# One turn of a software pipeline reordered: top-8 searches at its end, decoding at the start of the next, one-hot rows made a turn ahead

## The chip, the cores and the metric

The kernel runs on one core of one Trainium2 chip. Its time is the device time of one execution in microseconds (us). Each execution covers the whole layer, for 4096 tokens, from the inputs in HBM to the output in HBM.

## The reference

The layer has two parts, each added to its input with a gate (tanh of a scalar):

```python
x = x + tanh(g_xattn) * xattn(layernorm(x), ctx)      # 16 heads of 16, 64 keys, causal, softmax
h = silu(layernorm(x) @ W_up.T + b_up) @ W_down.T + b_down        # 256 -> 1024 -> 128
q = h @ W_q.T                                                     # 2 x 8 heads x 64
sim = einsum('pbthn,hkpn->pbthk', q, keys)                        # 16 rows of 45 per token
scores, idx = top_k(sim, 8)
all_scores = sx[..., :, None] + sy[..., None, :]                  # 8 x 8 sums per head
sc, pk = top_k(all_scores, 8); indices = ix * 45 + iy at pk       # 64 experts per token, of 2048
z = silu(einsum('btd,bthkd->bthk', h, down_embed[indices]) * softmax(sc))
x = x + tanh(g_ffn) * einsum('bthk,bthkd->btd', z, up_embed[indices])
```

The kernel never fetches a chosen expert's row. It computes h against all 2048 experts (a table of 128 rows r by 16 columns c), picks 64 values for each token with one-hot matrices, and spreads the 64 coefficients back into the same table before one dense product with `up_embed`.

## The kernel before

The 4096 tokens are 32 tiles of 128. The work on a tile is cut in five stages, and a turn i of the pipeline works on five tiles at once: L (tile i: load, first layernorm), A (i-1: attention), Fw (i-2: up and down projections, dense product z, similarities), B (i-3: router) and Ct (i-4: gather, coefficients, output). 36 turns are written out; 28 in the middle have all five stages. `turn(L, A, Fw, B, Ct, side)` exists once for each engine and is the order in which that engine takes its work. Engines meet through one semaphore for each step (`S["name"]`); a step waits with `wait(name)` for its own tile's count, with `free(name)` for the previous tile's. Nothing reorders the queues: a waiting instruction holds all that stands behind it on its engine.

What the texts below name:

- TensorE (PE): `up` L858, values L941, `gather(k)` L827 for k = 0 to 3 (16 pairs of tokens each: 48 matmuls of 32 columns, z in three bf16 parts against the one-hot rows `hot_rT`, into two PSUM banks in turn, so `gather(2)` waits for VectorE to have copied bank 0, `gather(3)` for bank 1), `scores` L868 between `gather(0)` and `gather(1)`, `probs_T` L901, down projection L960, `dense` L883, `scatter(k)` L845, output projection of the attention L997 (`wo_pe`), the product with `up_embed` L1004, the transposes L1010 of the second layernorm's result (`xn2_ok`) and L1018 of the router's columns and weights (`sm_pe`), and, opening the next turn, the transposes L919 of the first layernorm's result (`xn_ok`).
- VectorE (DVE): one-hot columns `hot_c` L630; `hot_T(part)` L602, which turns broadcast expert rows into the one-hot `hot_rT`; `gathered(k)` L589; `scores_max` L617; `up_silu` L623; coefficients `uc` L610; searches: `top` L798 (16 maxima over 45), `sums` L669, `best` L682, `besti` L691 and `topi` L702 (the indices); decoding: `ab_i` L731 to `r_h` L773 and `dif` L762, which turn found positions into expert numbers; `sm_in` L776 to L787 (softmax and what is transposed in L1018); `x1` L718 and the second layernorm's statistics to L728; `xn` L752 (second layernorm), `xn` L793 (first one); `x1k` L803, the turn's last.
- ScalarE (ACT): copies out of PSUM, tanh and exp; `top_rep` L541 and `ex` L544 serve the decoding, `sm_ok` L553 to L558 copies the result of L1018.
- GpSimd (POOL): `zl` L362 and `zll` L365 (the low bf16 parts of z), and two small powers, `rstdb` L368 and `rstd` L371, for the two layernorms.
- SyncE (SP) issues all DMAs on one queue: `xt`, `ct` in; the router's rows `r_h` out to HBM (L313); their broadcast to 128 partitions (L321, two of 1024 KB); the transposes of `hot_rT` to `hot_r` for the scatter (L309); the output (L326).

Before the change a turn ends on VectorE with decoding, `top` and `x1k`; `r_h` goes to HBM and comes back broadcast at the start of the next turn, where `hot_T(0)` and `hot_T(1)` wait for it, ahead of `gathered(0)`.

Of the kernel before, what the change touches and what calls it, by code (L numbers as in the profile page):

```python
# [27 lines left out]
SLOTS = RH * K8  # L28
# [9 lines left out]
def flamingo_layer(nc, x, ctx_512, g_xattn, g_ffn, Wq, Wkv, Wout, W_up, b_up, W_down, b_down, W_r,  # L38
# [10 lines left out]
    with es:  # L49
# [3 lines left out]
        def sem(name):  # L53
# [129 lines left out]
            "uc0 uc1 uc2 w_pe0 w_pe1 w_pe2 w_pe3 w_sb0 w_sb1 w_sb2 w_sb3 out_pe y_ok y_out0 y_out1 settled"  # L183
        ).split()}

        class Tile:

            def __init__(self, eng, t, count, pair):  # L190
                self.eng, self.t, self.pair, self.count = eng, t, pair, count
                self.later = not isinstance(t, int)

            def wait(self, name):
                self.eng.wait_ge(S[name], self.count(1))

            def wait_apart(self, name):

                self.wait(name)
                self.eng.sem_inc(S["settled"], 1)  # L200

            def wait_dma(self, name, n=1):

                self.eng.wait_ge(S[name], 16 * n * self.count(1))
# [4 lines left out]
            def free(self, name, n=1):  # L209
                if self.later or self.t > 0:  # L210
                    self.eng.wait_ge(S[name], n * self.count(0))

            def free_apart(self, name, n=1):
                if self.later or self.t > 0:
                    self.eng.wait_ge(S[name], n * self.count(0))
                    self.eng.sem_inc(S["settled"], 1)

            def free2(self, name, apart=False):
                if self.later or self.t > 1:
                    self.eng.wait_ge(S[name], self.count(-1))  # L220
                    if apart:
                        self.eng.sem_inc(S["settled"], 1)

            def free_dma_side(self, name):
                if self.later or self.pair > 0:
                    self.eng.wait_ge(S[name], 16 * self.pair)
# [3 lines left out]
        def one_turn(eng, turn, i):  # L230

            tiles = [Tile(eng, i - d, lambda k, t=i - d: t + k, (i - d) // 2) if 0 <= i - d < TILES else None
                     for d in range(DEPTH)]
            turn(*tiles, (i - 1) % 2)
# [61 lines left out]
        def _(sp):  # L296
            def turn(L, A, Fw, B, Ct, side):
                if L:
                    ls = 1 - side
                    L.free2("x1_ok", apart=True)  # L300
                    sp.dma_start(xt[:, ls, :], x_d[bass.ds(L.t, 1), :, :].rearrange("a p d -> p (a d)")).then_inc(S[f"x_in{ls}"], 16)
                    L.free2("xT_pe", apart=True)
                    sp.dma_start(ct[:, ls, :], ctx_d[bass.ds(L.t, 1), :, :].rearrange("a p d -> p (a d)")).then_inc(S[f"ctx_in{ls}"], 16)
                if Ct:
                    Ct.free_apart("w_pe3")
                    for part in range(2):
                        qs = slice(part * Q // 2, (part + 1) * Q // 2)
                        Ct.wait_apart(f"hotrT{part}")
                        sp.dma_start_transpose(hot_r[:, qs, :], hot_rT[:, qs, :].rearrange("r q s -> r (q s)")).then_inc(S[f"hotr_in{part}"], 16)  # L309
                if B:  # L310
                    B.wait_apart("rh_ok")
# [3 lines left out]
                    sp.sem_inc(S["settled"], 1)  # L315
                    B.free_apart("g_pe3")
                    for part in range(2):
                        B.free_apart(f"hotr_in{part}", 16)
                    for part in range(2):
# [3 lines left out]
                                     ).then_inc(S[f"rows_in{part}"], 16)  # L323
                if Ct:
                    Ct.wait_apart("y_ok")
                    sp.dma_start(out_d[bass.ds(Ct.t, 1), :, :].rearrange("a p d -> p (a d)"), x1k[:, 1 - side, :])\  # L326
                        .then_inc(S[f"y_out{1 - side}"], 16)
# [26 lines left out]
        def _(pool):  # L354
            def turn(L, A, Fw, B, Ct, side):
                if B:

                    B.wait("z_sb3")
                    B.free2("g_pe3")
                    if Ct:  # L360
                        Ct.wait("uc2")
                    nc.gpsimd.tensor_tensor(zl[:, side, :, :], z[:, side, :, :], top_half(z[:, side, :, :]), ALU.subtract).then_inc(S["zl_ok"], 1)  # L362
                if B:
                    B.wait("zl_ok")
                    nc.gpsimd.tensor_tensor(zll[:, side, :, :], zl[:, side, :, :], top_half(zl[:, side, :, :]), ALU.subtract).then_inc(S["zll_ok"], 1)  # L365
# [3 lines left out]
                if L:  # L369
                    L.wait("eps_ok")  # L370
                    nc.gpsimd.tensor_tensor(rstd[:, :], veps[:, :], minus_half[:, :], ALU.pow).then_inc(S["rstd_ok"], 1)  # L371
# [43 lines left out]
        def _(act):  # L415
            def turn(L, A, Fw, B, Ct, side):
# [57 lines left out]
                if A:  # L474
# [62 lines left out]
                if B:  # L537

                    B.wait("top_i")
                    B.free("pick_ok")  # L540
                    copy(top_rep[:, :, :, :], topi[:, :, :].rearrange("p l a -> p a l").unsqueeze(3).to_broadcast([128, K8, 2 * RH, K8]), "rep_ok")  # L541
                    B.wait("dif_ok")
                    B.free("p_ok")
                    nc.scalar.activation(ex[:, :, :], dif[:, :, :], ACT.Exp).then_inc(S["ex_ok"], 1)  # L544
# [4 lines left out]
                if B:  # L549

                    B.wait("sm_pe")
                    B.free2("hotc")
                    for half in range(2):  # L553
                        rows, cols = slice(half * 64, half * 64 + 64), slice(half * Q, half * Q + Q)
                        src = bG1[rows, 0:256].rearrange("p (n t) -> p n t", n=2)
                        nc.scalar.activation(c_sm[rows, side, :, :], src[:, 0, cols].unsqueeze(2).to_broadcast([64, Q, 2]), ACT.Copy)
                        last = nc.scalar.activation(p_sm[rows, side, :], src[:, 1, cols], ACT.Copy)
                    last.then_inc(S["sm_ok"], 1)  # L558
# [17 lines left out]
        def _(dve):  # L576
            def turn(L, A, Fw, B, Ct, side):
# [20 lines left out]
                def hot_T(part):  # L598

                    qs = slice(part * Q // 2, (part + 1) * Q // 2)  # L600
                    Ct.wait_dma(f"rows_in{part}")
# [26 lines left out]
                if Ct:  # L628
# [37 lines left out]
                if B:  # L666

                    B.wait("top_v")
                    nc.vector.tensor_tensor(sums[:, :, :, :],  # L669
                                            top[:, 0:RH, :].unsqueeze(3).to_broadcast([128, RH, K8, K8]),  # L670
                                            top[:, RH:2 * RH, :].unsqueeze(2).to_broadcast([128, RH, K8, K8]), ALU.add).then_inc(S["sums_ok"], 1)
# [6 lines left out]
                if B:  # L678

                    B.wait_apart("sums_ok")  # L680
                    for h in range(RH):
                        last = nc.vector.max(best[:, h, :], sums[:, h, :, :].rearrange("p a b -> p (a b)"))  # L682
                    last.then_inc(S["best_v"], 1)
# [4 lines left out]
                if B:  # L688
                    B.wait_apart("best_v")
                    for h in range(RH):  # L690
                        last = nc.vector.max_index(besti[:, h, :], best[:, h, :], sums[:, h, :, :].rearrange("p a b -> p (a b)"))  # L691
                    last.then_inc(S["best_i"], 1)
# [5 lines left out]
                if B:  # L698

                    B.wait_apart("top_v")  # L700
                    for l in range(2 * RH):
                        last = nc.vector.max_index(topi[:, l, :], top[:, l, :], sims[:, side, l, :])  # L702
                    last.then_inc(S["top_i"], 1)
                if L:

                    L.wait_dma_side(f"x_in{1 - side}")
                    nc.vector.bn_stats(st6[:, :], xt[:, 1 - side, :]).then_inc(S["stats"], 1)
                if L:
                    L.wait_apart("stats")
                    nc.vector.bn_aggr(mv[:, :], st6[:, :]).then_inc(S["stats2"], 1)  # L710
                if L:
                    L.wait("stats2")
                    nc.vector.tensor_scalar(veps[:, :], mv[:, 1:2], EPS, None, ALU.add).then_inc(S["eps_ok"], 1)
                if A:

                    A.wait("wo_pe")
                    A.free2("x1k_ok")
                    nc.vector.scalar_tensor_tensor(x1[:, side, :], bD[:, 0:DM], gates[:, 0:1], xt[:, side, :],  # L718
# [358 lines left out]
```

## Time and profile before

| | us |
|---|---|
| median of 3 runs | 1368.43 (1367.81 to 1371.82) |
| the profiled execution | 1370.69, its span 1368.9 |
| busy: TensorE, VectorE, ScalarE, GpSimd | 1238.8, 1020.6, 653.0, 289.0 |
| mean granted TensorE clock | 0.955 of 2.4 GHz |

The span runs from the first instruction to the last; some 1.8 us lie around it. In the pipeline's middle a turn is read from one `hot_c` on VectorE to the next.

### The profile page before, as it was taken

Reading aid. Unit: us, or ns where it says so; the run is one execution under the profiler, and the core shown is the slowest. Engines: PE = TensorE matmul, PEld = TensorE weight load, DVE = VectorE, ACT = ScalarE, POOL = GpSimd, SP = SyncE. Lnnn points to the kernel's source line nnn. Section 1 sums busy time; section 2 is a strip of 40 time slices with the busy share of each in tenths; the row PEclk is TensorE's granted clock in tenths of the full one; section 3 lists DMA queues with packets and bytes.
Section 4 is the critical chain, followed back from the end, with each engine's and each line's share of the span. In section 5 each row is a group of like instructions: output and inputs, shape, how many; then the busy total and the mean of one; then the engine's idle time right before and its main releaser. Section 6 shows DMA issues by size and latency. Waiting matters only on the chain.

```text
span 1368.9 us, 47081 instructions
## 1 busy us (share of the span) xinstructions
PE 1238.8 (90%) x18876; PEld 1101.5 (80%) x18876; DVE 1020.6 (75%) x4298; ACT 653.0 (48%) x1866; POOL 289.0 (21%) x151
## 2 busy tenths in 40 slices
PE   5778999999999999999999999999999999999755
PEld 3666888888888888888888888888888888888644
DVE  1437878886787878778878787787888778877873
ACT  3455544554554455555454554554545545554210
POOL 1220222220122222112222220222222112222220
PEclk9989999999999999999999999999999999999968
DMA  7005433565542455555443565544345565444455
GB/s 188 6 6 130 119 91 74 120 134 134 134 122 83 75 124 134 134 134 122 106 116 65 130 134 133 134 114 112 98 81 134 134 134 129 110 112 86 106 124 123
DMA packets 300319, 153.30 MB, mean 112 GB/s; under 512 B 278111, under 2 KB 291271, under 8 KB 291911
## 3 DMA queue, kind: packets, MB, share of 16 engines
q1 hardware_dynamic: 300103, 150.29, 47.6%
q8 instruction: 151, 2.47, 0.7%
q14 instruction: 65, 0.53, 0.1%
HBM read 78.44 MB, written 4.72 MB: 61 GB/s over the span
## 4 chain that ended last, share of the span: by engine, by line
DVE 40%; PE 25%; DMA 21%; issue 11%; SPq 2%; ACT 1%; DVEq 0%; POOL 0%; POOLq 0%
DMA hot_rT<-expert_rows 16%; DVE uc L610 7%; PE bank L960 6%; DVE topi L702 6%; PE bank L841 4%; DMA expert_rows<-r_h 4%; DVE picked L589 3%; DVE besti L691 3%; DVE smax L617 3%; PE bank L854 2%; DVE best L682 2%; PE bank L910 2%; PE bank L864 2%; PE bank L891 2%; DVE eq L740 2%
## 5 line engine op out<-in xcount | busy, mean ns | idle before, releaser
L362 POOL TENSOR_TENSOR zl<-z 128x2048 f32<-128x2048 f32 x32 | 115.3, 3602 | 916.0 <-DVE uc L610 916.0
L1004 PE MATMUL bank<-ue,coef 128*128 128x256 f32 x1024 | 226.5, 379 | 1.4 <-ACT coef L418 1.4
L841 PEld LDWEIGHTS bank<-z,hot_rT 128*128 128x128 bf16 x2048 | 156.8, 96 | 72.1 <-DVE picked L589 26.9
L1004 PEld LDWEIGHTS bank<-ue,coef 128*128 128x128 f32 x1024 | 192.1, 190 | 26.4 <-ACT coef L418 1.6
L841 PE MATMUL bank<-z,hot_rT 128*128 128x32 bf16 x2048 | 167.4, 178 | 45.9 <-DVE picked L589 27.3
L602 DVE TENSOR_SCALAR hot_rT<-hot_rT,p_iota 128x4096 bf16<-128x4096 bf16 x64 | 82.3, 1286 | 161.2 <-DMA hot_rT<-expert_rows 161.2
L854 PE MATMUL bank<-uc,hot_r 128*128 128x32 bf16 x6144 | 164.5, 177 | 24.1 <-DVE uc L610 16.4
L854 PEld LDWEIGHTS bank<-uc,hot_r 128*128 128x128 bf16 x6144 | 161.5, 96 | 29.9 <-issue 29.3
L841 PE MATMUL bank<-zll,hot_rT 128*128 128x32 bf16 x2048 | 166.1, 177 | 3.4 <-issue 3.4
L841 PE MATMUL bank<-zl,hot_rT 128*128 128x32 bf16 x2048 | 166.1, 177 | 2.7 <-issue 2.7
L841 PEld LDWEIGHTS bank<-zl,hot_rT 128*128 128x128 bf16 x2048 | 157.7, 97 | 3.5 <-issue 3.5
L841 PEld LDWEIGHTS bank<-zll,hot_rT 128*128 128x128 bf16 x2048 | 157.3, 96 | 2.5 <-issue 2.5
L453 ACT ACTIVATE P<-bank,smax 128x64 f32<-128x64 f32 x512 | 108.6, 363 | 75.8 <-DVE smax L617 75.8
L891 PEld LDWEIGHTS bank<-hT,deT 128*128 128x128 f32 x1024 | 127.2, 192 | 17.0 <-ACT hT L513 8.1
L891 PE MATMUL bank<-hT,deT 128*128 128x128 f32 x1024 | 133.5, 279 | 1.0 <-ACT hT L513 0.5
L610 DVE TENSOR_TENSOR uc<-hot_c,u_h 64x1024 bf16<-64x1024 bf16 x192 | 131.6, 685 | 3.3
L864 PE MATMUL bank<-xn2T,WupT 128*128 128x128 f32 x1024 | 128.6, 280 | 0.3 <-ACT xn2T L418 0.3
L418 ACT ACTIVATE coef<-bank 128x512 f32<-128x512 f32 x128 | 76.5, 597 | 103.8 <-PE bank L854 103.8
L864 PEld LDWEIGHTS bank<-xn2T,WupT 128*128 128x128 f32 x1024 | 123.4, 197 | 0.6 <-ACT xn2T L418 0.5
L365 POOL TENSOR_TENSOR zll<-zl 128x2048 bf16<-128x2048 f32 x32 | 115.3, 3602 | 2.5
L589 DVE TENSOR_TENSOR picked<-bank,hot_c 64x256 f32<-64x256 f32 x256 | 107.5, 420 | 10.7 <-PE bank L841 7.1
L418 ACT ACTIVATE z<-bank 128x512 f32<-128x512 f32 x128 | 76.5, 597 | 81.1 <-PE bank L891 81.1
(140 smaller groups left out, 2161.4 us busy)
## 6 DMA issues: line engine op xcount, KB each, us to landing
hot_rT<-expert_rows SPq DMA_DIRECT2D x64, 1024.0 KB, 6.2
xt<-in_x SPq DMA_DIRECT2D x32, 128.0 KB, 7.1
out<-x1k SPq DMA_DIRECT2D x32, 128.0 KB, 7.2
ue<-in_L_ffn_up_embed SPq DMA_DIRECT2D x1, 2048.0 KB, 16.3
ct<-in_ctx SPq DMA_DIRECT2D x32, 32.0 KB, 6.7
z<-in_L_ffn_W_up SPq DMA_DIRECT2D x1, 1024.0 KB, 8.8
expert_rows<-r_h SPq DMA_DIRECT2D x64, 8.0 KB, 1.8
hot_r<-hot_rT SPq DMA_TRANSPOSE x64, 8.2
```

The lines of the kernel that those rows point to most:

```text
L362: nc.gpsimd.tensor_tensor(zl[:, side, :, :], z[:, side, :, :], top_half(z[:, side, :, :]), ALU.subtract).then_inc(S["zl_ok"], 1)
L365: nc.gpsimd.tensor_tensor(zll[:, side, :, :], zl[:, side, :, :], top_half(zl[:, side, :, :]), ALU.subtract).then_inc(S["zll_ok"], 1)
L418: nc.scalar.activation(dst, src, ACT.Copy, scale=scale).then_inc(S[done], 1)
L453: last = nc.scalar.activation(P[:, h, :], bS[half][:, SEQ * n:SEQ * n + SEQ], ACT.Exp, bias=smax[:, h:h + 1])
L589: last = nc.vector.tensor_tensor(picked[rows, k % 2, :, :], bG[k % 2][rows, :].rearrange("s (q h c) -> s q h c", q=16, h=2)[:, :, half, :] ...
L602: nc.vector.tensor_scalar(hot_rT[:, qs, :], hot_rT[:, qs, :], p_iota[:, 0:1], None, ALU.is_equal).then_inc(S[f"hotrT{part}"], 1)
L610: last = nc.vector.tensor_tensor(uc[rows, n, :, C * half:C * half + C].rearrange("s q (c b) -> s q c b", b=2), hot_c[rows, :, :].rearrange ...
L841: last = mm(bG[k % 2][:, 32 * (q - 16 * k):32 * (q - 16 * k) + 32], hot_rT[:, q, :], part.rearrange("r (h q) c -> r h q c", h=2)[:, :, q, ...
L854: last = mm(bG[k % 2][:, 32 * (q - 16 * k):32 * (q - 16 * k) + 32], hot_r[:, q, :], uc[:, n, q, :], start=(n == 0), stop=(n == 2))
L864: last = mm(bS[n][:, 128 * m:128 * m + 128], WupT[:, k, 128 * c:128 * c + 128], xn2T[:, k, :], start=(k == 0), stop=(k == 1))
L891: last = mm(bS[n % 2][:, 128 * m:128 * m + 128], deT[:, R * c:R * c + R], hT[:, :], start=True, stop=True)
L1004: last = mm(bG0[:, 0:DM], coef[:, c, :, :].rearrange("r h q -> r (h q)"), ue[:, c, :], start=(c == 0), stop=(c == C - 1))
```

## The change

The order of the turn is changed on every engine; no operation on data is added or removed.

- VectorE: after `hot_c` come `dif` and the whole decoding to `r_h`, ahead of `up_silu(0)` and `gathered(0)`. `hot_T` is no longer there: it now stands in stage B, behind the statistics of the second layernorm, for the tile that is gathered one turn later. `top` and `sums` follow the attention's `xn` L696, now in stage Fw; then `sm_in`, statistics, `x1`, `hot_T(0)`, `hot_T(1)`, both `xn`; then, still in Fw, `best`, `besti`, `topi`; last `x1k`.
- SyncE: the transposes to `hot_r` move from Ct to B, behind the broadcast of the same tile; they wait for `hotrT` and `w_pe3`. The output store is behind them.
- GpSimd: the powers come first; `zl` and `zll` move from B to Fw and wait for `z_sb3`, `sums_ok`, `xn2_ok` and `xn_ok` in place of `uc2`.
- ScalarE: `top_rep` goes between the copies for the transposes and `up_bias(0)`, `ex` behind `up_tanh(0)`, `sm_ok` ahead of `xn2T`.
- TensorE: the transposes L1018 go ahead of the product L1004, into another bank (`bT`), and L1010 waits for `sm_ok`. `gather(1)` no longer waits for `sm_ok`.
- A counter semaphore `settled`, increased after some waits on VectorE and SyncE, is gone.

```diff
 # SyncE
-                if Ct:
-                    Ct.free_apart("w_pe3")
-                    for part in range(2):
-                        qs = slice(part * Q // 2, (part + 1) * Q // 2)
-                        Ct.wait_apart(f"hotrT{part}")
-                        sp.dma_start_transpose(hot_r[:, qs, :], hot_rT[:, qs, :].rearrange("r q s -> r (q s)")).then_inc(S[f"hotr_in{part}"], 16)
...
+                    B.free("w_pe3")
+                    for part in range(2):
+                        qs = slice(part * Q // 2, (part + 1) * Q // 2)
+                        B.wait(f"hotrT{part}")
+                        sp.dma_start_transpose(hot_r[:, qs, :], hot_rT[:, qs, :].rearrange("r q s -> r (q s)")).then_inc(S[f"hotr_in{part}"], 16)
 # GpSimd
-                if B:
-
-                    B.wait("z_sb3")
-                    B.free2("g_pe3")
-                    if Ct:
-                        Ct.wait("uc2")
...
+                if Fw:
+
+                    Fw.wait("z_sb3")
+                    Fw.free2("g_pe3")
+                    Fw.wait("sums_ok")
+                    if A:
+                        A.wait("xn2_ok")
+                    if L:
+                        L.wait("xn_ok")
+                    nc.gpsimd.tensor_tensor(zl[:, 1 - side, :, :], z[:, 1 - side, :, :], top_half(z[:, 1 - side, :, :]), ALU.subtract).then_inc(S["zl_ok"], 1)
 # ScalarE, behind the copies xT_sb and ctxT_sb
+                if B:
+
+                    B.wait("top_i")
+                    B.free("pick_ok")
+                    copy(top_rep[:, :, :, :], topi[:, :, :].rearrange("p l a -> p a l").unsqueeze(3).to_broadcast([128, K8, 2 * RH, K8]), "rep_ok")
                 if Fw:
                     up_bias(0)
                     up_tanh(0)
+                if B:
+                    B.wait("dif_ok")
+                    B.free("p_ok")
+                    nc.scalar.activation(ex[:, :, :], dif[:, :, :], ACT.Exp).then_inc(S["ex_ok"], 1)
 # VectorE, the start of the turn
-                    hot_T(0)
+                if B:
+                    B.wait("best_v")
+                    B.free("ex_ok")
+                    nc.vector.tensor_tensor(dif[:, :, :], best[:, :, :], best[:, :, 0:1].to_broadcast([128, RH, K8]),
...
                 if Fw:
                     up_silu(0)
                 if Ct:
-                    hot_T(1)
                     gathered(0)
 # VectorE, the end of the turn
+                if B:
+                    hot_T(0)
+                    hot_T(1)
                 if L:
                     L.wait("rstd_ok")
                     L.free("xT_pe")
...
+                if Fw:
+
+                    Fw.wait("sums_ok")
+                    for h in range(RH):
+                        last = nc.vector.max(best[:, h, :], sums[:, h, :, :].rearrange("p a b -> p (a b)"))
+                    last.then_inc(S["best_v"], 1)
...
 # TensorE
                 if Fw:
                     dense(3)
+                if B:
+                    B.wait("rdup_ok")
+                    B.wait("p_ok")
+                    if A:
+                        A.wait("oT_sb")
+                    for n in range(2):
+                        last = nc.tensor.transpose(bT[:, 256 + 128 * n:384 + 128 * n], sm_in[:, n, :, :].rearrange("p a s -> p (a s)"), ident[:, :])
+                    last.then_inc(S["sm_pe"], 1)
```

## Rows read from the trace of the kernel before

**Rows 1.** The page's granted clock in 40 slices of the span, tenths.
```profile
PEclk9989999999999999999999999999999999999968
```

**Rows 2.** The page's chain that ended last, shares by engine.
```profile
DVE 40%; PE 25%; DMA 21%; issue 11%; SPq 2%; ACT 1%; DVEq 0%; POOL 0%; POOLq 0%
```

**Rows 3.** Waits, 156.3 to 1262.5 us: waiter <- cause: us in total, times, longest.
```profile
DVE hot_rT L602 <- DMA hot_rT<-expert_rows: 142.7, 56, 5.2
...
PE bank L841 <- DVE picked L589: 24.7, 28, 1.4
...
PE bank L919 <- ACT xn2T L418: 9.4, 27, 0.3
```

**Rows 4.** TensorE by turn: stretch, us, busy (instructions), granted clock, DMA share, GB/s.
```profile
634.30:672.00 37.70, 36.74 (x590) 1.00 0.53 122
...
sum 458.70, PE 442.04; mean PE 36.84
...
sum 647.50, PE 614.25; mean PE 38.39
...
156.30:1262.50 1106.20, 1056.30 (x16435) 0.97 0.51 116
```

**Rows 5.** Short stretches, all engines: PE, PEld, DVE, ACT, POOL busy, PEclk, DMA.
```profile
605.70:607.10 1.40, 0.06 (x2) 0.07 (x3) 1.35 (x4) 1.40 (x8) 0.00 (x0) 1.00 1.56 151
608.10:611.50 3.40, 3.40 (x28) 3.40 (x24) 2.35 (x7) 1.55 (x6) 0.00 (x0) 0.50 1.10 250
```

**Rows 6.** Timeline of TensorE: start, us, what [idle before <- releaser].
```profile
646.30 0.19 PE L841 MATMUL bank<-z,hot_rT 128*128 128x32 bf16 x1 [0.45 <-DVE picked L589]
...
661.73 1.11 PE L997 MATMUL bank<-WoT,oT 128*128 128x256 f32 x4
```

**Rows 7.** Timeline of VectorE in the same turn.
```profile
641.39 1.28 DVE L602 TENSOR_SCALAR hot_rT<-hot_rT,p_iota 128x4096 bf16<-128x4096 bf16 x1 [0.92 <-DMA hot_rT<-expert_rows]
642.59 0.85 DVE L589 TENSOR_TENSOR picked<-bank,hot_c 64x256 f32<-64x256 f32 x2
643.47 0.69 DVE L623 SCALAR_TENSOR_TENSOR up_act<-up_act,P 128x512 f32<-128x512 f32 x1
...
663.30 0.48 DVE L718 SCALAR_TENSOR_TENSOR x<-bank,gates,xt 128x256 f32<-128x256 f32 x1
...
664.68 0.18 DVE L731 TENSOR_SCALAR ab_i<-besti 128x64 uint32<-128x64 uint32 x1
...
667.06 0.41 DVE L752 TENSOR_SCALAR xn<-x,mvb,rstdb 128x256 f32<-128x256 f32 x1
...
668.74 0.21 DVE L776 TENSOR_REDUCE exs<-ex 128x8 f32<-128x64 f32 x1
```

**Rows 8.** Timelines of GpSimd and VectorE, where the two meet.
```profile
79.64 0.55 POOL L371 TENSOR_TENSOR rstd<-veps,minus_half 128x1 f32<-128x1 f32 x1
...
83.84 3.60 POOL L365 TENSOR_TENSOR zll<-zl 128x2048 bf16<-128x2048 f32 x1
...
80.23 3.68 DVE L793 TENSOR_SCALAR xn<-xt,mv,rstd 128x256 f32<-128x256 f32 x1
...
627.66 1.01 POOL L371 TENSOR_TENSOR rstd<-veps,minus_half 128x1 f32<-128x1 f32 x1
...
627.56 0.69 DVE L740 TENSOR_TENSOR eq<-ab_h,a_iota 128x1024 bf16<-128x1024 bf16 x1
```

**Rows 9.** One line's instructions on SP (ns min/median/max), and the page's DMA issues.
```profile
L309 SPq DMA_TRANSPOSE hot_r<-hot_rT x64: 4807/5398/5645, 124.0 to 1344.3; - x64
...
hot_rT<-expert_rows SPq DMA_DIRECT2D x64, 1024.0 KB, 6.2
```

**Rows 10.** Timeline of TensorE in the filling and in the last turn.
```profile
83.97 0.48 PE L919 MATMUL bank<-ident,xn 128*128 128x128 f32 x1 [3.34 <-DVE xn L793]
...
114.19 0.48 PE L1010 MATMUL bank<-ident,xn 128*128 128x128 f32 x1 [4.65 <-DVE xn L752]
...
1338.71 0.21 PE L841 MATMUL bank<-z,hot_rT 128*128 128x32 bf16 x1 [6.32 <-DVE hot_rT L602]
```

More of the change, by code:

```diff
@@ L209, in free, with free2 @@
             def free(self, name, n=1):
[L210 to L222, printed above, removed]
+                if self.t > 0:
+                    self.eng.wait_ge(S[name], n * self.t)
+            def free2(self, name):
+                if self.t > 1:
+                    self.eng.wait_ge(S[name], self.t - 1)
             def free_dma_side(self, name):
-                if self.later or self.pair > 0:
+                if self.pair > 0:
                     self.eng.wait_ge(S[name], 16 * self.pair)
@@ L355, in turn @@
             def turn(L, A, Fw, B, Ct, side):
-                if B:
-                    B.wait("z_sb3")
-                    B.free2("g_pe3")
-                    if Ct:
-                        Ct.wait("uc2")
[L362 to L365, printed above, removed]
+                if L:
+                    L.wait("eps_ok")
+                    nc.gpsimd.tensor_tensor(rstd[:, :], veps[:, :], minus_half[:, :], ALU.pow).then_inc(S["rstd_ok"], 1)
                 if A:
@@ L537, in turn @@
                 if B:
[L539 to L544, printed above, removed]
+                    B.wait("sm_pe")
+                    B.free2("hotc")
+                    for half in range(2):
+                        rows, cols = slice(half * 64, half * 64 + 64), slice(half * Q, half * Q + Q)
+                        src = bT[rows, 256:512].rearrange("p (n t) -> p n t", n=2)
+                        nc.scalar.activation(c_sm[rows, side, :, :], src[:, 0, cols].unsqueeze(2).to_broadcast([64, Q, 2]), ACT.Copy)
+                        last = nc.scalar.activation(p_sm[rows, side, :], src[:, 1, cols], ACT.Copy)
+                    last.then_inc(S["sm_ok"], 1)
                 if A:
@@ L677, in turn @@
                     coef_parts(2)
[L678 to L683, printed above, removed]
                 if A:
@@ L697, in turn @@
                                             rsum[:, :, :, :].to_broadcast([128, 8, 2, HD]), ALU.mult).then_inc(S["o_ok"], 1)
-                if B:
-                    B.wait_apart("top_v")
+                if Fw:
+                    Fw.wait("sim_sb1")
                     for l in range(2 * RH):
[L702 to L718, printed above, removed]
-                                                   ALU.mult, ALU.add).then_inc(S["x1_ok"], 1)
@@ new lines, in turn @@
+                        last = nc.vector.max(top[:, l, :], sims[:, 1 - side, l, :])
+                    last.then_inc(S["top_v"], 1)
+                if Fw:
+                    Fw.wait("top_v")
+                    nc.vector.tensor_tensor(sums[:, :, :, :],
+                                            top[:, 0:RH, :].unsqueeze(3).to_broadcast([128, RH, K8, K8]),
+                                            top[:, RH:2 * RH, :].unsqueeze(2).to_broadcast([128, RH, K8, K8]), ALU.add).then_inc(S["sums_ok"], 1)
@@ L793, in turn @@
                     nc.vector.tensor_scalar(xn1[:, :], xt[:, 1 - side, :], mv[:, 0:1], rstd[:, 0:1], ALU.subtract, ALU.mult).then_inc(S["xn_ok"], 1)
-                if Fw:
-                    Fw.wait_apart("sim_sb1")
+                if A:
+                    A.wait("lrstd_ok")
+                    A.wait("oT_pe")
+                    nc.vector.tensor_scalar(xn[:, :], x1[:, side, :], mvb[:, 0:1], rstdb[:, 0:1],
+                                            ALU.subtract, ALU.mult).then_inc(S["xn2_ok"], 1)
+                if Fw:
+                    Fw.wait("sums_ok")
+                    for h in range(RH):
+                        last = nc.vector.max(best[:, h, :], sums[:, h, :, :].rearrange("p a b -> p (a b)"))
+                    last.then_inc(S["best_v"], 1)
+                if Fw:
+                    Fw.wait("best_v")
+                    for h in range(RH):
+                        last = nc.vector.max_index(besti[:, h, :], best[:, h, :], sums[:, h, :, :].rearrange("p a b -> p (a b)"))
+                    last.then_inc(S["best_i"], 1)
+                if Fw:
+                    Fw.wait("top_v")
                     for l in range(2 * RH):
-                        last = nc.vector.max(top[:, l, :], sims[:, 1 - side, l, :])
-                    last.then_inc(S["top_v"], 1)
+                        last = nc.vector.max_index(topi[:, l, :], top[:, l, :], sims[:, 1 - side, l, :])
+                    last.then_inc(S["top_i"], 1)
                 if Ct:
@@ L1011, in turn @@
                     last.then_inc(S["x2T_pe"], 1)
-                if B:
-                    B.wait("rdup_ok")
-                    B.wait("p_ok")
-                    if Ct:
-                        Ct.wait("w_sb3")
-                    for n in range(2):
-                        last = nc.tensor.transpose(bG1[:, 128 * n:128 * n + 128], sm_in[:, n, :, :].rearrange("p a s -> p (a s)"), ident[:, :])
-                    last.then_inc(S["sm_pe"], 1)
             groups = list(weight_groups())
```

173 lines of the change are left out of this document (77 added, 96 removed).

## The prediction, made before the change was built

> **What bounds the kernel now.** I began with the chain that ended last, because it names candidates: VectorE 40%, TensorE 25%, DMA 21% [rows 2]. It can't price them. VectorE waits 142.7 us for the broadcast rows in the 28 full turns, in 56 waits [rows 3], and it is tempting to book these as the gain. So next I read the full turns by TensorE's busy time: 1056.3 of 1106.2 us [rows 4]. TensorE is the bound; it idles 49.9 us, 1.8 us a turn. The waits say where: 24.7 us, in each of the 28 turns, before `gather(3)`, for VectorE's copy of bank 1; 9.4 us for a copy by ScalarE at the seam of two turns [rows 3]. Third I looked at the clock, which the page shows barely under full [rows 1]. By turns it is two populations. Twelve keep the full clock and sum to 458.7 us, 38.2 each, with 36.84 busy; the sixteen others sum to 647.5, 40.5 each, with 38.39 busy for the same matmuls [rows 4]. In one of them TensorE is empty from 605.7 to 607.1 (0.06 us busy of 1.40) and then held at 0.50, 1.2 GHz, from 608.1 to 611.5 [rows 5]. I place the other falls in the same way, behind the wait of `gather(3)`, and read off that an idle of 1.4 us there is followed by a fall, one of 0.45 us, as in the turn from 634.3, is not. A late `gather(3)` is thus paid twice: once as idle, once as 38.39 - 36.84 = 1.55 us of slower matmuls.
>
> **Why `gather(3)` is late.** VectorE runs in order. `hot_T(1)` starts at 641.39, once its rows have landed; `gathered(0)` follows, at 642.59, then `up_silu(1)`, `scores_max` and `gathered(1)`, which lets `gather(3)` start at 646.30 [rows 6, 7]. The change takes both `hot_T` and the DMA wait out of this stretch and puts the decoding there.
>
> **The new turn, TensorE's own path.** The turn from 634.3 took 37.7 us; without its wait of 0.45 it is 37.25 [rows 4, 6]. Moving L1018 ahead of L1004 adds and removes nothing on TensorE, as long as `sm_in` is done, which now stands before `x1`.
>
> **The new turn, the loop through VectorE and GpSimd.** This is the term that I take most care with, since here the change adds waits. I start at the end of the attention's output projection, 661.73 + 1.11 = 662.84, which releases `x1`:
> - `x1` and statistics: 664.68 - 663.30 = 1.38 [rows 7].
> - `hot_T` twice: 642.59 - 641.39 = 1.20 for the first, 1.28 for the second [rows 7]; at 3.86 both are done. Their rows have long landed: the broadcast is issued once `gather(3)` is over, some 16 us earlier, and takes 6.2 us [rows 9].
> - `rstdb` on GpSimd is asked for just as `hot_T` begins. A `rstd` took 0.55 us alone but 1.01 beside VectorE's `eq` and ended at 628.67, 0.42 behind the end of `eq` at 628.25 [rows 8]. So I let it end at 3.86 + 0.42 = 4.3; `xn` L752 takes 0.41 [rows 7]: 4.7. GpSimd waits for this (`xn2_ok`).
> - `zl` and `zll`: 3.60 each [rows 8] and 0.08 between, an estimate: with a hop of 0.1 they run from 4.8 to 12.1.
> - VectorE meanwhile does `best`, `besti`, `topi`, `x1k`, some 5.9 us (estimated from their groups in the trace), free of GpSimd, and reaches `hot_c` at about 10.6. Here GpSimd's work meets VectorE's. An `xn` of 0.41 us took 3.68 when it came under `zl`, and ended at 83.91, as `zll` started at 83.84 [rows 8]. I take `hot_c` to be held in this way until 12.1. Nearest bounds: not held at all (0), held to the end of `zll` (1.5 us); I take the second, for the rows show both engines waiting for each other.
> - `hot_c`, like `eq` 0.69: 12.8. Decoding: 668.74 - 664.68 = 4.06, less the 0.33 of the `xn` inside it, 3.7: 16.5. `up_silu(0)`, 0.69 less overlap, 0.6: 17.1 [rows 7].
> - from `gathered(0)` to the start of `gather(3)`: 646.30 - 642.59 = 3.71 [rows 6, 7]: 20.8.
> - from `gather(3)` to the end of the output projection: 662.84 - 646.30 = 16.54 [rows 6]: 37.4.
> So this loop, 37.4, is just above TensorE's path of 37.25. With 0.1 for semaphore hops the turn is 37.5. The idle before `gather(3)` is then some 0.25 us, below the 0.45 at which the clock stayed full. Full turns: 28 x 37.5 = 1050, against 1106.2: -56.
>
> The Trainium skill, "SBUF — State Buffer", section "Who interferes with whom", puts it as a rule that a VectorE instruction with two SBUF inputs contends with a GpSimd one that reads SBUF, and that the loser blocks for all of the other's instruction. Of such an instruction held on VectorE's side no row here is at hand (the 3.68 us are a tensor_scalar); by the rule `hot_c` is held, and the sum is 37.5, without it 37.25.
>
> **Edits costed at nothing.** On ScalarE `top_rep` falls in the wait for `up(0)`; `ex` delays the copies for `scores` by some 0.3 us, with about 0.5 in hand. If GpSimd frees `hot_c` 1 us later than I have it, `dif` and `ex` make `scores` late. On SyncE the two transposes hold the queue for 2 x 5.4 = 10.8 us [rows 9], from `hot_T(0)` (2.6 on the scale above) to 13.4. Queued behind are the output store, the next `xt` and `ct`, and the wait for `r_h`, which comes at 16.5: 3 us in hand. The store frees `x1k` for ScalarE's copy ahead of the exponentials; it is issued at 13.4 and wanted at about 17. The transposes themselves are wanted by `scatter(0)` a whole half turn later. `zl` is finished a turn before it is needed. The removed increments of `settled` cost nothing that the profile counts.
>
> **Filling and emptying.** In the filling TensorE waits 3.34 us for the `xn` that `zl` held, and 4.65 for an `xn` behind indices and decoding [rows 10]. The first is ordered away, but `top` and `sums` now stand ahead of `x1`; in the second `hot_T` takes the decoding's place. I book -5, between -8 and 0. In the last turn TensorE waits 6.32 us for broadcast and `hot_T` [rows 10], in the one before about the same, in the third from last 2. With rows made a turn ahead I book -6, -5 and -3: -14, between -18 and -8; in the last but one the decoding fills part of the hole.
>
> **Sum.** 1370.7 (the profiled execution: span 1368.9 and 1.8 around it) - 56 - 5 - 14 = 1295.7. The median of the three runs is 2.3 below the profiled one; I forecast 1295.
>
> **Rivals.**
> - *TensorE's path alone binds.* `hot_c` and `dif` slip through ahead of the end of `zll`. Then the loop is 0.9 shorter, 36.5, the turn 37.2: 28 x 37.2 = 1042, total 1287. For it: nothing shown holds a tensor_tensor on VectorE. Against: `ab_i`, a tensor_scalar, comes right behind it. Chance 0.15.
> - *The wait before `gather(3)` stays long enough for the clock to fall.* If the loop is 38.2 or more, idle is 0.9 or more, and by the two populations the fall of 1.55 us comes back: 37.25 + 0.9 + 1.55 = 39.7, 28 x 39.7 = 1112, with filling and emptying 1358; if it falls in half of the turns, about 1330. For it: the margins above are tenths; the first layernorm, `rstdb` and `hot_T` compete for the same few hundred ns. Chance 0.18.
> - *Slower.* GpSimd's pair starts still later. The place is `rstdb`: VectorE can hold it through both `hot_T` and the `xn` L793 behind them, and `xn2_ok` then waits for it, `zl` for that, and next turn's decoding, `gathered(1)` and `gather(3)` for `zll`. Each us is one us of the turn, plus the fall of the clock. Slower by 0.3% needs 28 turns to sum to over 1106 + 19 + 4 = 1129, 40.3 each: 40.3 - 1.55 - 37.4 = 1.35 us more than summed. The rows give 0.4 for one `xn`, so I hold it for unlikely: at 2 us 28 x 41 = 1148, total 1394. Chance 0.04.
> - *Nothing comes of it*: the same with about 1.2 us more than summed, 1368. Chance 0.03.
>
> **How the numbers follow.** Forecast 0.60, its own range 1284 to 1316 (turns of 37.2 to 38, falls of the clock in none to a few, filling and emptying -26 to -8). The range for 8 in 10 goes down to 1280, for a free `hot_c` with the full gain at the ends, and up to 1340, which takes in the second rival where the clock falls in half of the turns. 0.3% is about what a measurement of this kernel can tell from no change. Faster by more than that: 0.60 + 0.15 + 0.18 = 0.93, of which I take 0.03 off, as 1358 is near the line, and get 0.90; within it 0.05; slower 0.05.
>
> **What would show it.** Right: the wait of TensorE for `picked` falls from 24.7 us to under 10; the clock is full in most turns; turns from `hot_c` to `hot_c` of about 37.5; VectorE no longer waits for the broadcast; `hot_c` (or `dif`, `ab_i`) of over 1.5 us, ending with `zll`; no wait for TensorE at `hot_rT` in the last turns. Wrong: idle of 0.9 us or more in the gathers with clock 0.50 behind it; ScalarE waiting for `dif` or `topi` and TensorE for `scores`; SyncE late for `r_h`.

## The result, and the profile after

The changed kernel takes 1295.5 us (median of 4 runs, 1295.0 to 1296.1), the kernel before 1368.8 beside it: a ratio of 0.946, interval 0.945 to 0.948. I had forecast 1295. The total is right; two of its three terms are not, and their errors cancel by luck. I read the new profile in the order of the prediction: chain and clock, full turns, waits, then the place where GpSimd and VectorE meet, then both ends.

The page of the changed kernel: granted clock in 40 slices, and the chain that ended last (before: [rows 1, 2]).
```profile
PEclk9897999999999999999999999999999999999877
PE 86%; DVE 6%; issue 4%; ACT 2%; POOL 1%; DMA 0%; SPq 0%; POOLq 0%; DVEq 0%; ACTq 0%
```
VectorE's share of the chain fell from 40% to 6% and the DMAs' from 21% to nothing; TensorE has it nearly alone. The page books VectorE as busy for 1075.0 us and GpSimd for 330.7, 54 and 42 more than before for the same work: for the most part time in which one held the other, that is, an instruction that had been started lasted until one on the other engine had ended.

The 28 full turns of the changed kernel, columns as in [rows 4], then its waits in the same stretch, as in [rows 3].
```profile
161.50:1199.70 1038.20, 1020.48 (x16437) 1.00 0.50 124
```
```profile
DVE x L746 <- PE bank L981: 55.2, 28, 2.7
...
POOL zl L352 <- DVE xn L767: 24.0, 28, 0.9
...
PE bank L903 <- ACT xn2T L401: 15.3, 27, 0.6
```
1038.2 us for 28 turns, 37.1 each, at the full clock throughout; before it was 1106.2 at 0.97 [rows 4]. The wait of TensorE for `picked`, 24.7 us before [rows 3], has no line any more, nor has the wait of VectorE for the broadcast. What is left to TensorE is the seam of two turns, where it waits for ScalarE's copy of the second layernorm's transposed result: 0.57 us each time; before it was 0.35 [rows 3]. The transposes L1018 used to stand in this gap, behind L1010; the change took them away, and the idle is 0.22 longer. Timeline of TensorE before, at the end of the turn from 634.3:
```profile
670.47 0.38 PE L1010 MATMUL bank<-ident,xn 128*128 128x128 f32 x2
670.69 0.38 PE L1018 MATMUL bank<-ident,sm_in 128*128 128x128 f32 x2
671.42 0.41 PE L919 MATMUL bank<-ident,xn 128*128 128x128 f32 x2 [0.35 <-ACT xn2T L418]
```
VectorE now waits for TensorE, 2 us a turn ahead of `x1`.

SyncE's queue, a wait from 156.3 to 1262.5 us, and its transposes (ns min/median/max), as in [rows 9].
```profile
SPq L290 <- DVE r_h L658: 68.2, 30, 3.4
```
```profile
L304 SPq DMA_TRANSPOSE hot_r<-hot_rT x64: 4788/4908/5377, 117.0 to 1259.4; - x64
```
SyncE still waits 2.3 us a turn for `r_h` behind the transposes; I had 3 us in hand.

Timelines of VectorE and GpSimd of the changed kernel, around the end of a turn (`hot_c` at 606.46 opens the next one).
```profile
596.27 0.48 DVE L746 SCALAR_TENSOR_TENSOR x<-bank,gates,xt 128x256 f32<-128x256 f32 x1 [1.89 <-PE bank L981]
597.54 2.47 DVE L586 TENSOR_SCALAR hot_rT<-hot_rT,p_iota 128x4096 bf16<-128x4096 bf16 x2
597.71 2.35 POOL L342 TENSOR_TENSOR rstdb<-vepsb,minus_half 128x1 f32<-128x1 f32 x1 [2.70 <-DVE vepsb L756]
600.92 3.60 POOL L352 TENSOR_TENSOR zl<-z 128x2048 f32<-128x2048 f32 x1 [0.86 <-DVE xn L767]
604.60 3.60 POOL L354 TENSOR_TENSOR zll<-zl 128x2048 bf16<-128x2048 f32 x1
606.46 2.28 DVE L614 TENSOR_TENSOR hot_c<-c_sm,col_iota 128x1024 bf16<-128x1024 bf16 x1
...
616.07 0.85 DVE L573 TENSOR_TENSOR picked<-bank,hot_c 64x256 f32<-64x256 f32 x2
```
This is the loop as I had written it down. `rstdb`, a 128x1 operation, is held through both `hot_T` (2.35 us, end 600.06, where the two `hot_T` end at 600.01). `best`, `besti` and `topi` on VectorE run under `zl` unhindered: 0.21, 0.22 and 0.20 us each, as before the change. `hot_c` comes under `zll` and takes 2.28 us instead of 0.7; it ends at 608.74, behind the end of `zll` at 608.20. From the start of `x1` to the end of this `picked` it is 616.92 - 596.27 = 20.65 us; I had 20.8.

The filling: timelines of GpSimd, VectorE and TensorE in the changed kernel (before: [rows 10]), and last the `xn` that stood beside the same clearing before the change.
```profile
37.06 5.22 POOL L389 MEMSET uc<- 128x6144 bf16 x1
37.14 5.28 DVE L767 TENSOR_SCALAR xn<-x,mvb,rstdb 128x256 f32<-128x256 f32 x1 [0.44 <-POOL rstdb L342]
42.48 0.69 PE L1004 MATMUL bank<-ident,xn 128*128 128x128 f32 x2 [7.51 <-DVE xn L767]
...
118.83 0.69 PE L1004 MATMUL bank<-ident,xn 128*128 128x128 f32 x2 [4.61 <-DVE xn L767]
```
```profile
38.85 5.28 DVE L793 TENSOR_SCALAR xn<-xt,mv,rstd 128x256 f32<-128x256 f32 x1
```
The clearing of `uc` (a memset), done once, now starts just ahead of the first `xn` of the second layernorm and holds it for 5.28 us; TensorE waits 7.51. Before the change the same memset held the other `xn` L793 just as long, but that one was wanted only at 52.4, so it cost nothing. The 4.65 us of [rows 10] are still there, as 4.61.

Put together, by `hot_c`: the first full turn starts at 161.5 (before 156.3), the 28 take 1038.2 (1106.2), the rest 93.5 (106.4). That is +5.2, -68.0 and -12.9, -75.7 in all, from a span of 1368.9 to one of 1293.2. In a second profile of the changed kernel, below, the first full turn starts at 162.6, so the +5.2 is good to about 1 us.

### The profile page after: what moved, and what is told of

It reads as the page before. It is cut to its first block, busy times and chain, and to the rows that moved or that the text cites. A ratio compares the mean times of both kernels' runs of the same rounds, so it can differ in the third digit from the quotient of the medians.

```text
span 1293.2 us, 46670 instructions
## 1 busy us (share of the span) xinstructions
PE 1203.8 (93%) x18876; PEld 1073.7 (83%) x18876; DVE 1075.0 (83%) x4298; ACT 646.9 (50%) x1866; POOL 330.7 (26%) x151
## 4 chain that ended last, share of the span: by engine, by line
PE 86%; DVE 6%; issue 4%; ACT 2%; POOL 1%; DMA 0%; SPq 0%; POOLq 0%; DVEq 0%; ACTq 0%
PE bank L996 16%; PE bank L838 12%; PE bank L825 11%; PE bank L875 9%; PE bank L848 8%; PE bank L944 4%; PE bank L960 4%; PE bank L883 3%; PE bank L863 3%; PE bank L915 3%; PE bank L925 2%; PE bank L894 2%; PE bank L981 2%; PE bank L912 1%; PE bank L858 1%
## 5 line engine op out<-in xcount | busy, mean ns | idle before, releaser
L339 POOL TENSOR_TENSOR rstd<-veps,minus_half 128x1 f32<-128x1 f32 x32 | 17.6, 549 | 738.8 <-DVE veps L741 738.8
L825 PE MATMUL bank<-z,hot_rT 128*128 128x32 bf16 x2048 | 161.9, 177 | 7.8 <-DVE picked L573 6.4
L825 PE MATMUL bank<-zll,hot_rT 128*128 128x32 bf16 x2048 | 161.1, 177 | 1.2 <-issue 1.2
L825 PE MATMUL bank<-zl,hot_rT 128*128 128x32 bf16 x2048 | 161.1, 177 | 0.0
```

The lines of the kernel that those rows point to most:

```text
L825: last = mm(bG[k % 2][:, 32 * (q - 16 * k):32 * (q - 16 * k) + 32], hot_rT[:, q, :], part.rearrange("r (h q) c -> r h q c", h=2)[:, :, q, ...
```

## The experiments

All times are medians; ratios are to the kernel before on the same chip, whose medians were 1370.7, 1366.2 and 1370.0 in the three groups (no_settled, zll_short, x2T_early, zll_short_x2T; then delay1, delay3, hotT_first, memset_first; then all3, x2T_mem, pool_back, after_again). Turns are means over the 28 full ones, from `hot_c` to `hot_c`; in the changed kernel this is 37.08, most turns taking 37.0 and a few 37.3 to 37.8. The changed kernel run once more beside the last group gave 1295.3 (4 runs), ratio 0.947 [0.943, 0.950].

> The changed kernel itself, on the chip of the three others, to compare them with. As measured: 1295.5, within 3 us; full turns of 37.0 to 37.1 at the full clock, start to the second turn 56.

The time came as expected, with full turns of 37.06; the second turn starts 1.7 us later than in the first profile, so single us of the filling aren't read from one profile. The changed kernel's two medians, 1295.5 and 1295.3, agree, and the variants are compared with it directly, though it ran beside the last group only; the kernel before moved by up to 4.5 us from group to group, so smaller differences between groups are not read from the times alone.

**The counter alone (no_settled).** The kernel before, without the increments of `settled`:
```diff
                 self.wait(name)
-                self.eng.sem_inc(S["settled"], 1)
```
(and in three more places)

> The kernel before, with only the increments of the counter semaphore settled taken out (the waits stay). Theory A, the gain is the order of the work: no difference, 1368 within 0.3%. Rival R, the increments cost time on VectorE's and SyncE's queues, some 10 of them a turn on VectorE: up to 0.1 us each on a queue that is late for gather(3), 1 us a turn and fewer falls of the clock, 1340 or less.

Measured: 1357.2 (10 runs), ratio 0.992 [0.989, 0.994], between the two expectations. So the counter was worth 0.8%, and what I had put at nothing is some 11 us. The kernel without it and the changed kernel differ by the order of the work and the waits that go with it: this is worth the other 62 us, from 1357.2 to 1295.5. Two of its turns and the sum of all, TensorE:
```profile
238.50:275.60 37.10, 36.52 (x588) 1.00 0.53 125
314.90:355.30 40.40, 38.63 (x590) 0.96 0.49 115
159.90:1255.70 1095.80, 1048.52 (x16411) 0.98 0.50 117
```
The first of them is a turn of the old order with no stall in the gathers: 37.1, which I had put at 37.25 by way of a turn that still had the increments. Others still stall, and 13 of the 28 fall to half the clock for a while, against 16 with the counter. In the changed kernel itself the counter was not put back.

**GpSimd's part undone (pool_back).**
```diff
-                if Fw:
-                    Fw.wait("z_sb3")
...
+                if B:
+                    B.wait("z_sb3")
+                    B.free2("g_pe3")
+                    if Ct:
+                        Ct.wait("uc2")
```

> The change with its GpSimd part undone: zl and zll again for the router's tile, behind the coefficients (uc2), then the two powers. Everything else as in the changed kernel. Theory (a VectorE instruction with two SBUF inputs that meets zl or zll is held to its end, and here uc, sums, sm_in and the first layernorm's statistics stand beside the pair): the last uc or sums is held up to 3.6 us, sm_in or rstd again, x1 starts 1 to 3 us later, turn 38 to 41 with falls of the clock in some, time 1320 to 1400; hot_c takes 0.69. Rival (it is room on VectorE that counts, 3.8 us idle a turn, half of it ahead of x1): the held time is covered by the 1.9 us wait ahead of x1, hot_c is no longer held, turn 36.9 to 37.1, time 1290 to 1297.

Measured: 1345.6 (4 runs), ratio 0.983 [0.979, 0.987]; 50 us of the gain hang on GpSimd's part, the place of `zl` and `zll` and with it the order of the two powers. By the marks of `hot_c` 36 of the 50 are in the full turns, 11 ahead of them and 4 behind. Timelines of GpSimd and VectorE, and one of the waits over 27 full turns:
```profile
579.36 3.93 POOL L346 TENSOR_TENSOR zll<-zl 128x2048 bf16<-128x2048 f32 x1
580.11 3.26 DVE L722 CAST sm_in<-rc_i 128x128 f32<-128x128 uint32 x1
...
595.03 0.68 DVE L612 TENSOR_TENSOR hot_c<-c_sm,col_iota 128x1024 bf16<-128x1024 bf16 x1
```
```profile
PE bank L989 <- DVE sm_in L722: 20.0, 26, 0.8
```
`hot_c` runs free (0.68), but a cast of 128x128, 0.19 us in the changed kernel, is held for 3.26 until `zll` has ended. `sm_in` is late, and TensorE waits for it ahead of the transposes that the change had moved forward: 0.8 us a turn. The turn is 38.40 (27 of the 28). The theory holds in place and direction, though the clock stayed full. The rival, that the 1.9 us which VectorE waited ahead of `x1` cover what is held there, falls: that wait is gone, and the turn is longer. But the place isn't the only thing that differs. In `sums` (1.82 instead of 0.69) and `sm_in` some 4.2 us a turn are held here, against 1.6 in `hot_c` of the changed kernel, 2.6 more, which is more than the 1.9 that were spare. How much of the 1.3 us is the place and how much the amount was not separated.

**Is it the loop or TensorE's path?** Three kernels. zll_short computes `zll` for 16 of the 128 tokens only (0.62 us instead of 3.60) and clears the rest once at the start, so that the lowest part of z is left out for 112 tokens:
```diff
-zll[:, 1 - side, :, :], zl[:, 1 - side, :, :], top_half(zl[:, 1 - side, :, :])
+zll[:, 1 - side, 0:16, :], zl[:, 1 - side, 0:16, :], top_half(zl[:, 1 - side, :, :])[:, 0:16, :]
```
x2T_early puts TensorE's transposes of the second layernorm's result inside the output's sum, so that their copy is ready at the seam:
```diff
                     for c in range(C):
+                        if A and c == 13:
+                            second_T()
                         last = mm(bG0[:, 0:DM], coef[:, c, :, :].rearrange("r h q -> r (h q)"), ue[:, c, :], start=(c == 0), stop=(c == C - 1))
...
-                    for k in range(2):
-                        last = nc.tensor.transpose(bT[:, 128 * k:128 * k + 128], xn[:, 128 * k:128 * k + 128], ident[:, :])
```
zll_short_x2T does both.

> The changed kernel, with GpSimd's zll on 16 of 128 tokens only (the rest of zll stays zero, so the lowest part of z is left out for 112 tokens). GpSimd then ends some 3.1 us earlier and no longer holds hot_c. Theory A, TensorE's own path binds (37.0 us a turn, 0.6 of it idle at the seam): hot_c falls from 2.28 to 0.69 us and the time stays at 1295, within 0.3%. Rival L, the loop through VectorE and GpSimd binds (x1 to gathered(1) 20.65 us, gather(3) to the end of the output projection 16.3): the turn loses up to 0.5 us, about 1283.

> The changed kernel, with the two transposes of the second layernorm's result (L1004 of the changed kernel) put ahead of the last three of the 16 steps of the product with up_embed, so that ScalarE copies them while TensorE still multiplies: the idle of 0.56 us at the seam of two turns goes. Theory A (TensorE's path binds, the loop has slack of 0.5 us or more): 28 x 0.55 = 15 us less, 1280. Rival L (the loop binds or is equally long): no gain, the idle comes back before gather(3), 1293 to 1296.

> Both edits: zll on 16 of 128 tokens (lowest part of z left out for the others), transposes of the second layernorm's result ahead of the last three steps of the product with up_embed. If path and loop are equally long, as I now think (37.0 and 36.95), neither edit alone gains much and both together take the seam away: 36.45 us a turn, 1280. If TensorE's path alone binds: the same 1280, but x2T_early alone has it already. If something else binds: 1295.

Measured: 1294.9, 1294.4 and 1274.0 (ratios 0.946 [0.942, 0.950], 0.947 [0.943, 0.951], 0.932 [0.928, 0.935]). TensorE in the 28 full turns of each:
```profile
164.90:1203.10 1038.20, 1019.07 (x16410) 1.00 0.50 124
```
```profile
162.00:1197.70 1035.70, 1017.92 (x16409) 1.00 0.51 124
```
```profile
162.70:1178.60 1015.90, 1013.16 (x16410) 1.00 0.52 127
```
With the short `zll`, `hot_c` takes 0.70, but the turn stays at 37.08, and VectorE idles 5.4 us instead of 3.9. With the early transposes the seam closes, but 0.5 us of idle comes back in the gathers, and the turn is 36.99. Both together give 36.28, where 36.45 was expected. So the loop and TensorE's path with its seam are equally long, 37.0, and only shortening both shows.

**What lateness costs (delay1, delay3).** One or three additions of 128x1024, whose result nobody uses, on VectorE ahead of `gathered(0)`. Each takes 0.69 us, but the next starts before it has quite ended (three take 1.89 from the first start to the last end), so one lengthens VectorE's work by 0.60 us and three by 1.8, less than the 0.7 and 2.15 of the expectations:
```diff
                 if Ct:
+                    for n in range(1):
+                        nc.vector.tensor_tensor(pad[:, n, :], a_iota[:, :, :].rearrange("p a s -> p (a s)"), a_iota[:, :, :].rearrange("p a s -> p (a s)"), ALU.add)
                     gathered(0)
```

> The changed kernel, with one more VectorE instruction of 128x1024 bf16 (0.69 us, result unused) ahead of gathered(0). Loop and TensorE's path are equally long, so theory A: each turn gets 0.7 us longer, as idle ahead of gather(3), and the clock stays full, as it did before the change at such idle: 1295 + 28 x 0.7 = 1314. Rival S (there is slack): under 1303. Rival C (the clock falls at any idle): 28 x 1.55 more, 1358.

> The same with three such instructions, 2.15 us. Theory A, an idle of over 1 us ahead of gather(3) brings the falls of the clock back, each worth 1.55 us: 1295 + 28 x 2.15 = 1355 for the idle alone, and with a fall in 16 to 28 turns 1380 to 1398. Rival N, the falls have another cause than this idle: 1355, clock 1.00 in the full turns.

Measured: 1311.7 (ratio 0.961 [0.957, 0.966]) and 1380.2 (1.012 [1.007, 1.017]). With one, the turn is 37.58, TensorE idles 0.4 us ahead of `gather(3)` and the clock stays full. With three it idles 1.4, and the turns at the full clock take 38.77. Less what was put in, both give 37.0 for the loop, as x2T_early does. Of delay3: the idle in front of `gather(3)` in the timeline, then TensorE in the stretches of that idle, behind it, and of the fall, and last two whole turns.
```profile
177.81 0.19 PE L828 MATMUL bank<-z,hot_rT 128*128 128x32 bf16 x1 [1.36 <-DVE picked L574]
```
```profile
176.60:178.00 1.40, 0.19 (x7) 1.00 0.00 0
178.00:179.20 1.20, 1.20 (x50) 1.00 0.05 14
179.20:182.60 3.40, 3.40 (x18) 0.51 0.72 246
```
```profile
246.60:285.30 38.70, 36.61 (x587) 1.00 0.48 116
285.30:325.70 40.40, 38.32 (x589) 0.96 0.46 118
```
The old pattern is back: empty for 1.4 us, busy at the full clock for a moment, then 3.4 us at 1.2 GHz. It costs 38.32 - 36.61 = 1.7 us of slower matmuls (I had 1.55). 1.8 us of VectorE work a turn, 50 in 28 turns, cost 85 us in all, more than the change had brought. But the same idle of 1.4 stands in every turn and only 19 of 28 fall, mostly two of three.

**The filling (memset_first).**
```diff
-            start(pool, turn, 1)
             step(nc.gpsimd.memset(uc[:, :, :, :], 0.0))
+            start(pool, turn, 1)
```

> The changed kernel, with GpSimd's memset of uc (5.22 us, once, at the start) ahead of its turn 1 instead of behind it. In the changed kernel the second layernorm's xn of turn 1 took 5.28 us under this memset, where before the change it had come first, and turn 2 began 3.2 us later. Theory A: that xn takes 0.41 us again and the time falls by 4 to 5 us, 1291. Rival: the start is set by the weights' DMAs anyway, no difference.

Measured: 1290.9 (1289.7 to 1292.6), 4.4 us below the changed kernel and 4.2 below hotT_first, which ran beside it and still has the memset where it was (its own ratio, 0.946 [0.942, 0.951], can't tell that much). VectorE and TensorE at the place of the 5.28 and 7.51 us:
```profile
37.28 0.41 DVE L767 TENSOR_SCALAR xn<-x,mvb,rstdb 128x256 f32<-128x256 f32 x1 [0.44 <-POOL rstdb L342]
...
37.75 0.69 PE L1004 MATMUL bank<-ident,xn 128*128 128x128 f32 x2 [2.64 <-DVE xn L767]
```
The second turn starts at 51.5 instead of 56.1. Of these 4.6 us less is left where the first full turn starts: 159.3, against 161.5 and 162.6 in the two profiles of the changed kernel and 156.3 before the change. So the memset accounts for 2 to 3 us of the +5.2, and what makes the rest was not run.

**Both `hot_T` ahead of `x1` (hotT_first, x2T_mem, all3).** So that they run where VectorE waited for TensorE:
```diff
+                if B:
+                    hot_T(0)
+                    hot_T(1)
                 if A:
                     A.wait("wo_pe")
...
-                if B:
-                    hot_T(0)
-                    hot_T(1)
```
x2T_mem is x2T_early with memset_first; all3 is hotT_first on top of these two.

> The changed kernel, with both hot_T ahead of x1, where VectorE waits 1.9 us in each turn for the attention's output projection. The loop gets some 1.9 us shorter, rstdb no longer waits for hot_T (2.35 us to 0.55) and hot_c is no longer held to the end of zll. TensorE's path stays at 37.0 us, so theory A: full turns unchanged, some 2 us less in the filling (TensorE waits there 4.61 us for an xn behind hot_T): 1291 to 1295. Rival L (the loop alone binds): 28 x 0.5 = 14 us less, 1281.

> The same without the move of hot_T: the transposes inside the output's sum and the memset ahead of the first powers. Theory (the loop is still 37.0): turn 36.95 to 37.0, time 1288 to 1292. Rival (the seam alone is what the combined kernel gains from): turn 36.4, time 1275.

> Three edits at once: both hot_T ahead of x1, the transposes of the second layernorm's result inside the output's sum, the memset of uc ahead of the first powers on GpSimd. Theory (TensorE's path with the seam, 37.0, and the loop through x1, rstdb, zl, zll and the held hot_c, 37.0, are equally long; each alone gives nothing, both together do): hot_T is taken out of the loop (-2.4), the seam idle out of the path (-0.6), so the turn falls to 36.3 to 36.5, 28 turns to 1016 to 1022, and with 4 us less in the filling the time is 1270 to 1280. Rival (VectorE as a whole or the held hot_c sets the turn whatever stands in front of x1): turn 37.0, time 1290.

Measured: hotT_first 1295.1 (ratio 0.949 [0.944, 0.953]), x2T_mem 1287.9 (0.942 [0.938, 0.946]), all3 1268.2 (1267.1 to 1270.4; 0.927 [0.923, 0.930]). The move of `hot_T` gives nothing while the seam is open and 19.7 us once it is closed. Two links of the first expectation failed: `hot_c` stays held (2.30), since it still meets `zll` (the `hot_T` now hold `rstd` for 2.35 and not `rstdb`, for which VectorE waits 0.44); and in the filling the wait of 4.61 became 5.14, since there VectorE had no wait ahead of `x1` to put the `hot_T` in. Of all3, 28 full turns, then GpSimd and VectorE at the start of a turn:
```profile
158.20:1175.70 1017.50, 1015.34 (x16438) 1.00 0.52 127
```
```profile
592.62 3.60 POOL L354 TENSOR_TENSOR zll<-zl 128x2048 bf16<-128x2048 f32 x1
594.48 2.28 DVE L614 TENSOR_TENSOR hot_c<-c_sm,col_iota 128x1024 bf16<-128x1024 bf16 x1
```
A turn is 36.3 and TensorE is busy for all but 2.2 of 1017.5 us. `hot_c` is still held for 2.28 us, and it costs nothing. all3 leaves nothing out and beats the changed kernel by 27 us; it came 2 us below its range.

## Why the prediction was right, and where it was not

- **TensorE is the bound, not VectorE.** Right. The 142.7 us of waits for the broadcast are gone, and the full turns gained 68.
- **A late `gather(3)` is paid twice.** Right: delay3 brings back idle and fall, 1.7 us for the fall against 1.55. Too simple was the bound, "idle is 0.9 or more": in delay3 9 of 28 turns don't fall after 1.4 us, and in no_settled this turn idles 2.1 us at one place in the gathers and keeps the full clock (TensorE, the turn and the idle in it):
```profile
275.60:314.90 39.30, 36.65 (x588) 1.00 0.50 117
287.30:289.40 2.10, 0.03 (x2) 1.00 0.56 104
```
The idle ahead of the gather doesn't decide alone; what else does stays open.
- **The loop.** Right link by link, but not as the one bound: at 37.0 it is as long as TensorE's path, as zll_short and x2T_early show. `hot_c` was the link on which rows were wanting. It took 2.28 us; the rule of the Trainium skill ("SBUF — State Buffer", "Who interferes with whom") that I had quoted for it holds here. The rival by which it slips through (1287) falls: it is held in every full turn.
- **The turn of 37.5.** This is the first mis-sized term: 37.0 to 37.1, so -68 instead of -56. From `x1` to `gathered(1)` it was 20.65 instead of 20.8; from there to the end of the output projection (at 633.24) 16.32 instead of 16.54; the hop of 0.1 that I added at the end was not there. TensorE's own path, 37.25, came from a turn of the old kernel; the old order without its counter already shows 37.1. And that the move of L1018 "adds and removes nothing" was wrong by the 0.22 us that the seam grew, 6 us in 28 turns, though the path is shorter than I had it even so.
- **"The removed increments of `settled` cost nothing".** Wrong: 0.8% in the old order. It may be part of the 12 us by which the full turns came out better, but that was not run. The reordering alone is worth 62 us of the 73.
- **Filling, -5, between -8 and 0.** Wrong, also in its bounds: +5.2. I listed what TensorE waited for before and asked whether each goes, and not what the new order puts beside `xn` L752, there a `memset` that had been harmless. memset_first gives back 4.6 us at the second turn and 2 to 3 at the first full one; the rest of the miss stays open. The wait of 4.65 that I let shrink stayed at 4.61, since both `hot_T` and the held `rstdb` took the decoding's place in full.
- **Emptying, -14.** Right: -12.9, with no wait for `hot_rT`.
- **`rstdb`, the place of the rival "slower".** The holding was real: 2.35 us, through both `hot_T` but not through the `xn` behind them; I had let it end 0.4 behind them. It ended 0.05 behind. So this rival was right about the place and had no price. pool_back shows the neighbour that did: with GpSimd's order left as it was, the same change brings 24 us instead of 75.
- **The rival with falls of the clock.** It didn't come: the clock is full in all 28. For falls in half of the turns its own numbers give 28 x 38.9 = 1090 and a total of 1335, not "about 1330".
- **The edits at nothing on SyncE and ScalarE.** No line of the full turns speaks against them: TensorE waits for neither `scores` nor a transfer.

So the total of 1295.7 owes its closeness to -12 in the full turns and +10 in the filling. That they cancel is luck; the direction and the mechanism in the full turns are not.

## What to carry to other kernels

A wait that is long in the sum of waits is worth only what reaches the engine that bounds; find the few tenths of a us that it waits, and ask whether they also cost it its clock. When work is moved, list for each engine what will run beside it, the one-time work of the first turns too, for a small operation under a long one on the other engine can take the long one's time. When a shortened path gives nothing, look for a second path of the same length and shorten both: here two edits that gave 0.4 and 0.9 us alone, no more than the noise, gave 21 together.

## What the runs showed of the hardware

- An instruction on GpSimd held simple VectorE instructions to its end or just past it: a cast of 0.19 us took 3.26 under `zll`, a tensor_scalar of 0.41 took 5.28 under a memset of 5.22, a tensor_tensor of 0.69 took 2.28 and ended 0.54 behind `zll`. Not held were max (0.21), find_index (0.20 and 0.22) and, with one input in PSUM, `x1k` (0.47), all under `zl` or `zll`. The other way round, a power over 128x1, 0.67 us alone, took 2.35 under two `hot_T`: it was not done between the two, but 0.05 us behind the second.
- Increments of a semaphore that nobody waits on were worth 0.8% of the whole (no_settled).
- An idle of 0.4 us in the gathers (delay1), or of 0.8 and 0.6 at two other places of a turn (pool_back), left the clock at 2.4 GHz in all full turns; behind one of 1.4 us it fell to 1.2 GHz in 19 of 28 turns (delay3), and behind one of 2.1 us in a turn of no_settled it did not fall.
